# Second attention: half of the softmax row sums begun on GpSimd by three halving additions

## The reference, cut to what matters

```python
x = x + _L1_xattn_ref(_layernorm(x, axis=-1), ctx_768, ...)

qh = (q @ Wq + bq).reshape(b, lq, H, HD).transpose(0, 2, 1, 3)     # H = 16, HD = 8
kh = (kv @ Wk + bk).reshape(b, lkv, H, HD).transpose(0, 2, 1, 3)
vh = (kv @ Wv + bv).reshape(b, lkv, H, HD).transpose(0, 2, 1, 3)
scores = jnp.einsum('bhqd,bhkd->bhqk', qh, kh) * scale[0]
attn = jax.nn.softmax(scores, axis=-1)
out = jnp.einsum('bhqk,bhkd->bhqd', attn, vh)
out = out.transpose(0, 2, 1, 3).reshape(b, lq, DQ)
return out @ Wo + bo
```

## Time and profile before

| what | us |
|---|---|
| median of 3 runs | 1208.37 (1203.44 to 1216.89) |
| the profiled execution's own time | 1209.02 |
| its span, first to last instruction | 1207.7 |
| busy in the span: PE, DVE, ACT, POOL | 911.1, 770.4, 431.2, 438.6 |

### The profile page before, as it was taken

The page is one execution under the profiler, slowest core; times in us unless marked ns, Lnnn a source line. Parts: engine busy times, 40 slices in busy tenths (PEclk is TensorE's granted clock), DMA queues, the critical chain, the costliest instruction groups (busy, mean ns, idle before and its releaser), DMA issues. The chain is left out here.

```text
span 1207.7 us, 20885 instructions
## 1 busy us (share of the span) xinstructions
PE 911.1 (75%) x6494; PEld 678.4 (56%) x6494; DVE 770.4 (64%) x3188; ACT 431.2 (36%) x1047; POOL 438.6 (36%) x759
## 2 busy tenths in 40 slices
PE   0957667764939996367791389996648999999998
PEld 0734334331926544264560266664527888888887
DVE  7949999996338872801112589998465565565565
ACT  1444545442015652002120278885202232232232
POOL 5114766667264420314654555562222000000000
PEclk9965765665569996558895589998568999999999
DMA  8211111110040000014424000000000000000002
GB/s 166 64 33 31 38 35 36 36 34 13 2 172 18 19 26 9 1 27 81 87 75 150 11 2 2 3 2 2 2 0 1 1 1 0 1 1 1 1 9 62
DMA packets 66068, 37.84 MB, mean 31 GB/s; under 512 B 39482, under 2 KB 60083, under 8 KB 65460
## 3 DMA queue, kind: packets, MB, share of 16 engines
q1 hardware_dynamic: 63206, 32.31, 9.8%
q0 software_dynamic: 2048, 4.20, 2.1%
q10 hardware_dynamic: 718, 0.17, 0.1%
HBM read 26.11 MB, written 10.55 MB: 30 GB/s over the span
## 5 line engine op out<-in xcount | busy, mean ns | idle before, releaser
L1872 ACT ACTIVATE e_sg<-e_ps,vec 128x512 f32<-128x512 f32 x128 | 88.2, 689 | 211.4 <-PE e_ps L1854 211.4
L1907 DVE SCALAR_TENSOR_TENSOR e_hh<-e_ps,vec,e_sg 128x512 f32<-128x512 f32 x128 | 96.1, 750 | 50.5 <-ACT e_sg L1872 40.7
L1839 PEld LDWEIGHTS e_psy<-w_folded,e_hh 128*128 128x128 f32 x1024 | 123.9, 191 | 4.9
L1839 PE MATMUL e_psy<-w_folded,e_hh 128*128 128x128 f32 x1024 | 124.3, 275 | 0.0
L1899 DVE SCALAR_TENSOR_TENSOR X<-e_psy,gate,X 128x128 f32 (+1 forms) x256 | 72.4, 344 | 74.0 <-PE e_psy L1839 73.7
L1852 PE MATMUL e_ps<-e_XH,e_wh 128*128 (+1 forms) x256 | 105.9, 414 | 14.0 <-POOL e_wl L1884 14.0
L1853 PE MATMUL e_ps<-e_XL,e_wh 128*128 (+1 forms) x256 | 100.7, 393 | 0.0
L1854 PE MATMUL e_ps<-e_XH,e_wl 128*128 (+1 forms) x256 | 100.5, 393 | 0.0
L1884 POOL TENSOR_TENSOR e_wl<-w_folded,e_wh 128x512 fp32r<-128x512 f32 x8 | 10.3, 1293 | 220.2 <-DVE e_wh L1889 220.2
L1555 POOL TENSOR_SCALAR a_kb<-a_kr,a_m,a_bk 128x128 f32<-128x128 f32 x128 | 57.9, 452 | 55.2 <-issue 38.0
L758 DVE MATCH_REPLACE8 work<-m,work 128x64 f32<-128x64 f32 x384 | 75.7, 206 | 0.0
(11 more groups left out here) (367 smaller groups left out, 2184.7 us busy)
## 6 DMA issues: line engine op xcount, KB each, us to landing
toe<-s4d_kernel SPq DMA_DIRECT2D x64, 64.0 KB
planes<-rt_zeros SPq DMA_DIRECT2D x4, 1024.0 KB, 8.4
ew<-in_L_ffn_ew SPq DMA_DIRECT2D x16, 256.0 KB, 3.6
comb_y<-planes SPq DMA_DIRECT2D x16, 256.0 KB, 5.6
X<-in_x SPq DMA_DIRECT2D x4, 512.0 KB, 6.7
fold_wr<-in_L_ffn_W SPq DMA_DIRECT2D x16, 128.0 KB, 2.5
rows<-XT SPq DMA_DIRECT2D x8, 256.0 KB, 2.0
out_dram<-X SPq DMA_DIRECT2D x8, 256.0 KB, 2.3
```

Source lines behind the costliest of these rows:

```text
L1839: mm = pe.matmul(psy[j][:, k, :], hh[j][:, c, k * P:(k + 1) * P], G.w2[:, e, c, :], start=(c == 0 and k == 0), stop=(c == NC - 1), skip_gr ...
L1872: act.activation(sg[j][:, c, :], psh[0][c][:], ACT.Silu, bias=G.vec[:, k:k + 1]).then_inc(silu[c], 1)
L1907: dve.scalar_tensor_tensor(hh[j][:, c, :], psh[1][c][:], G.vec[:, k:k + 1], sg[j][:, c, :], ALU.add, ALU.mult).then_inc(hh_sb[c], 1)
```

## The change

POOL gets three additions per tile: it folds the exponentials of heads 0 to 7 from 64 numbers to 32, to 16 and to 8. They stand in POOL's slot between rc and kb. DVE's one sum over 16 heads of 64 numbers becomes two: 8 heads of 64 numbers straight from `pp`, and 8 heads of 8 numbers from POOL's result `h8`, for which it waits on the new semaphore `eighths`. `h32` and `h16` exist once, `h8` twice. Before it overwrites an `h8`, POOL waits for the sums of two tiles earlier. Arithmetic and results are otherwise the same.

```diff
+        h32, h16 = (C.sb(f"a1_h{n}", [P, 8, n], ctx=ctx) for n in (32, 16))
+        h8 = two("h8", [P, 8, 8])
...
                         pool.tensor_copy(rc[c.j][:], wide(ri[c.j][:].unsqueeze(2), [P, H1, DH1])).then_inc(s["rc"], 1)
                         pool.wait_ge(s["rc"], c.t + 1)
+                    if x.real():
+                        p = pp[x.j][:, 0:8, :]
+                        pool.wait_ge(s["exp"], 2 * x.t + 1)
+                        step.then(pool.tensor_tensor(h32[:], p[:, :, 0:32], p[:, :, 32:64], ALU.add))
+                        step.then(pool.tensor_tensor(h16[:], h32[:, :, 0:16], h32[:, :, 16:32], ALU.add))
+                        after(pool, s["sums"], x.t - 1)
+                        pool.tensor_tensor(h8[x.j][:], h16[:, :, 0:8], h16[:, :, 8:16], ALU.add).then_inc(s["eighths"], 1)
+                        pool.wait_ge(s["eighths"], x.t + 1)
                     if a.real():
...
                     if x.real():
                         dve.wait_ge(s["exp"], 2 * x.t + 2)
-                        dve.tensor_reduce(sm[x.j][:], pp[x.j][:], AX.X, ALU.add).then_inc(s["sums"], 1)
+                        dve.tensor_reduce(sm[x.j][:, 8:16], pp[x.j][:, 8:16, :], AX.X, ALU.add)
+                        dve.wait_ge(s["eighths"], x.t + 1)
+                        dve.tensor_reduce(sm[x.j][:, 0:8], h8[x.j][:], AX.X, ALU.add).then_inc(s["sums"], 1)
```

More of the change, by code:

```diff
@@ L1508, in second_attention @@
             "weights", "ready", "const_ps", "const", "zero", "qkv", "v_sb", "q_sb", "k_sb", "kb",
-            "scores", "max", "centred", "exp", "sums", "turned", "turned_sb", "inverse", "rc", "rt_sb", "o", "of", "y", "xc", "x", "pool")}
+            "scores", "max", "centred", "exp", "sums", "turned", "turned_sb", "inverse", "rc", "rt_sb", "o", "of", "y", "xc", "x", "pool", "eighths")}
         def vb_rows(j, odd):
```

## The result

The changed kernel takes 1226.16 us (median of 8 runs, 1222.61 to 1231.03) against 1209.21 us (median of 8, 1203.44 to 1217.75) for the kernel before. The ratio is 1.0123, with a 95% interval of 1.0084 to 1.0162: slower, clear of no change, though the interval leaves open whether by more than 1%. I had said 1222.0, 1.1% slower.

A forecast was written before the change was run, and what follows sets the result against it. DVE alone was taken to set the old 4.28 us slot, POOL the new one at 3.08 + 1.74 = 4.82; over 27 slots 14.6 us, less 1.0 in the tail, taking profiled 1209.0 to 1222.6, stated as 1222.0; range 1209 to 1234.

The forecast's parts named there:

- POOL becomes the bound: POOL's slot: 3.08 us of own work plus 1.74 of additions gives 4.82, against 3.88 that DVE would need.
- The bounds on either side of the price: Three additions on POOL, priced 1.74 us with waits: lower bound 1.51, upper 2.01, kept for reading pieces with gaps.
- one wait of 0.9 us: DVE in each slot: a sign that it idles ahead of the second sum, released by POOL.
- No collision with DVE: POOL's additions beside DVE: claimed to run at full speed, slot 4.82 us; 5.09 if they collided.
- 27 slots: Steady part, kb(4) to kb(31) on POOL: 27 slots of 4.82 instead of 4.28 us, kb(31) 14.6 us late.
- The tail: Stage end behind kb(31): POOL's slot 2.63 us under DVE's 3.88, giving back 1.0 of the 14.6 us.
- of(30): DVE near the stage's end: a sign, expected at about 849.0 us instead of 835.37, 13.6 late.
- The third rival: TensorE's clock falls from a 0.98 us idle in each slot: 25 us more, 1247 us; chance 0.05.
- The first rival's floor: Additions hide on POOL below 1.20 us: slot down to 4.03, 6.8 us gained, 1201.6; hidden, not slower, had chance 0.07.
- The fourth rival: DVE's wait for additions delays next kr: 3.1 us against 4.82, claimed to cost nothing; no separate chance.

The follow-up runs named there:

- e1: Changed kernel, but DVE sums all 16 heads itself and never reads POOL's three additions; slot 4.84 us, ratio 1.015 to the kernel before.
- e4: Changed kernel with POOL's three additions moved behind kb and ahead of the constant; slot 7.11 us, ratio 1.0661 to the kernel before.
- e2: Changed kernel without POOL's three additions, DVE's second short sum reading a constant tile of ones; slot 4.26 us, ratio 0.9989 to the kernel before.
- e5: As e2, with ScalarE's first exponential also moved behind kr and qt; slot 4.03 us, ratio 0.9939 to the kernel before.
- e9: Changed kernel with only POOL's first halving of eight heads, ScalarE's order as before; slot 4.26 us, ratio 1.0014 to the kernel before.
- e3: Changed kernel with POOL's addition of the constant row to X replaced by a bare semaphore increment; slot 4.50 us, ratio 1.0041 to the kernel before.
- e12: Changed kernel with ScalarE's first exponential moved behind kr and qt; slot 4.83 us, ratio 1.0115 to the kernel before.

## Why the prediction was right

- **POOL becomes the bound.** Right, and by the margin given. POOL's slot was put at 4.82 and is 4.85 us. The additions are 729, 461 and 320 ns where I had 727, 454 and 320, and 0.10 us instead of 0.08 stand between the last of them and kb. The bounds on either side of the price were not needed: read pieces of 32, 16 and 8 numbers with gaps cost what unbroken rows cost.
- **Where DVE waits.** I had named one wait of 0.9 us, ahead of the second sum. It is 0.38 us there and 0.36 ahead of mx, since TensorE's scores come late behind rc. That changes nothing in the sum, as DVE is not the bound.
- **No collision with DVE.** DVE's `dd` is 0.69 us as before and POOL's additions run at the price they had elsewhere. The Trainium skill's page SBUF — State Buffer, section Who interferes with whom, has it that a DVE instruction with one SBUF operand leaves GpSimd alone. The trace agrees: `dd` has a mean of 692 ns here and 691 before.
- **27 slots.** Right: kb(31) came 15.4 us later in the stage, 14.6 predicted; the difference is the 0.03 us per slot.
- **The tail.** Wrong in sign, by a microsecond: I had it give back 1.0 us, and it took 0.1 more. The step that failed is the one in which DVE goes on to the last maxima without a wait. In the first slot without projections TensorE waited 1.65 us for rc, and then its clock fell for some 3 us; the transposes took twice their time and DVE waited 1.94 us for scores (timelines of PE and DVE, and one window, columns as in the earlier trace rows):

```profile
847.98 0.33 PE L1614 MATMUL a_psx<-ident,a_rc 128*128 128x128 f32 x1 [1.65 <-POOL a_rc L1550]
...
849.37 1.92 PE L1641 MATMUL a_psp<-ident,a_pp 128*128 128x128 f32 x8
```

```profile
852.41 0.69 DVE L1707 TENSOR_REDUCE a_mx<-a_pss 128x8 f32<-128x512 f32 x1 [1.94 <-PE a_pss L1594]
```

```profile
850.00:852.50 2.50, 2.50 (x29) 1.41 (x29) 0.56 (x4) 1.36 (x3) 1.87 (x5) 0.54 0.00 0
```

e1 has the same slot after a like wait with the clock up (PE, a window, DVE). From that rc to this mx it takes 3.21 us there (845.80 to 849.01) and 4.78 here (847.63 to 852.41), so 1.57 us of the 1.94 are the clock:

```profile
846.15 0.33 PE L1614 MATMUL a_psx<-ident,a_rc 128*128 128x128 f32 x1 [1.64 <-POOL a_rc L1550]
```

```profile
848.00:850.00 2.00, 2.00 (x61) 1.26 (x59) 1.55 (x6) 1.43 (x3) 1.50 (x4) 1.00 0.00 0
```

```profile
849.01 0.69 DVE L1708 TENSOR_REDUCE a_mx<-a_pss 128x8 f32<-128x512 f32 x1 [0.42 <-PE a_pss L1594]
```

of(30), which I had named as a sign at 849.0, started at 858.80 us. Without the 7.05 us by which the stage began later that is 16.4 behind the 835.37 of before, where I had 13.6. The last X is only 15.5 late, since from 857.50 to 862.50 TensorE's clock was 1.00 here, while the kernel before had 0.57 in its window from 835.00 to 837.50.
- **The clock in the steady part.** The third rival did not come: 1.00 with a wait of 1.0 us in each of the slots. The Trainium skill's page TensorE: Matmul & The Clock Gate, section HAM oscillation — how this bites in real kernels, tells of a kernel whose array falls back to its slow clock with the wait of every tile. I wrote that its rule would make this rival the outcome, and that went too far: by the page's figures that kernel waits some 3 to 5 us per tile. The changed kernel's trace does not show such a fall in its steady slots; e4's, with waits of up to 3.13 us, shows it in part (0.67 to 0.84).
- **The first rival's floor was wrong.** I wrote that below a price of 1.20 us the slot would fall with the price, down to 4.03, and that work taken from DVE shortens the slot until another engine is as slow. Both miss the ring of two slots at 4.26. e2 shows it by leaving the additions out altogether (4.26), e5 by opening it (4.03), e9 by a cheap addition that gained nothing. The forecast did not rest on this step, as POOL's 4.85 lies above the ring, but a reader who had trusted the floor would have expected 5 us from e9 and got none.
- **The fourth rival** was priced from the last addition to kr at 3.1 us against 4.82 and cost nothing. e4 shows what it costs when the additions stand behind kb.

In the sum, two of my errors were small and had the same sign (0.8 us in the slots, 1.1 in the tail), which leaves the stage 15.5 us longer instead of 13.6. The medians differ by 17, with an interval of some 10 to 20, so the time alone could not tell 13.6 from 15.5; the slots can.

## What to carry to other kernels

Before work is moved to an engine that looks half idle, add up that engine's own slot with what follows each instruction, and compare it with the slot of the bound: 41% idle was here 1.20 us, and three small additions cost 1.77. When the busiest engine is relieved, look for rings that pass through several engines and more than one turn of the loop; a ring 0.02 us below the bound showed in no wait here, and an alternation of slots after the relief was its mark. Where an engine waits for something anyway, work placed ahead of that wait is hidden as far as the wait reaches, and the same work behind it may close a ring that costs more than the work itself (e4: 1.77 us of additions, 2.26 us per slot over the changed kernel).

## What the runs showed of the hardware that I had not expected

A semaphore increment on POOL without an instruction to carry it, with the wait for it, took 0.17 us more than the plain gap between two instructions (0.25 against 0.08, e3).

TensorE's granted clock, once up, stayed at its upper level through waits of 1.0 us in each of some 27 slots. What it does behind a longer wait the length of that wait does not settle. Behind 1.65 us it fell in the changed kernel (0.78 granted in the window of that wait, 0.54 in the next), and behind 1.62 in e12 (0.50 from 840.00 to 842.50), but behind 1.64 in e1 it stayed at 1.00. Behind 2.16 us it fell in the kernel before (0.75), but behind 2.09 in the changed kernel, at 856.98, it stayed at 1.00 from 857.50 to 862.50. Why it falls behind one wait and not behind another of the same length stays open.
